# Window attention's order, and random features with 32-column stationary tiles, in an eight-stage hybrid network

## The reference, cut to what matters

```python
q = l2norm(q) * qs; k = l2norm(k) * ksc
q, k = rotary_xpos(q, k)
sim = einsum('bhwid,bhwjd->bhwij', bq * 8.0, bk)   # own window of 64 and the one before
mask = (i < j) | (i > j + WINDOW) | (j == -1)
out = einsum('bhwij,bhwjd->bhwid', softmax(where(mask, -max, sim)), bv)
x = x + out @ wo
```

```python
logits = einsum('bhld,hdf->bhlf', k, W0) - 0.5 * sum(k * k, -1)
alpha = softmax(logits over all l and f of a head)
N = einsum('bhlf,bhld->bhfd', alpha, v); D = sum(alpha, l)
phi = softmax(einsum('bhld,hdf->bhlf', q, W0), -1)
out = einsum('bhlf,bhfd->bhld', phi, N) / (einsum('bhlf,bhf->bhl', phi, D) + 1e-6)
```

## Time and profile before

| | |
|---|---|
| median of 3 runs | 6596.02 us (6581.57 to 6598.25) |
| profiled execution | 6608.01 us, its span 6606.2 us |
| busy PE, DVE, ACT, POOL | 5725.1, 3415.3, 3359.1, 2531.4 us |
| mean granted TensorE clock | 0.935 of 2.4 GHz |

### The profile page before, as it was taken

One profiled execution on the slowest core, in us unless ns is written; L12 is line 12 of the kernel. 1 busy time (PEld: TensorE's weight loads), 2 busy tenths in 40 slices (PEclk: granted clock), 3 DMA queues, 4 the chain that ended last, 5 costly groups with the idle time before them and its releaser, 6 DMA issues. The chain is left out here.

```text
span 6606.2 us, 126709 instructions
## 1 busy us (share of the span) xinstructions
PE 5725.1 (87%) x46071; PEld 3420.8 (52%) x46071; DVE 3415.3 (52%) x4087; ACT 3359.1 (51%) x5004; POOL 2531.4 (38%) x1721
## 2 busy tenths in 40 slices
PE   6876888888878988988998988998898998998998
PEld 2432555555535544553444554553446775676776
DVE  4557999999835544553435544554542112543112
ACT  4545888888834543544444443554343334332433
POOL 1223999999905524550215533551220000000000
PEclk8997999999989998999998999999998999888999
DMA  0002111111011101110001111110000000000000
GB/s 39 1 0 77 31 32 31 31 30 32 28 42 39 38 19 33 38 32 0 1 2 39 38 26 26 38 38 26 1 0 6 0 0 0 0 0 0 0 0 13
DMA packets 119695, 137.07 MB, mean 21 GB/s; under 512 B 31713, under 2 KB 85089, under 8 KB 118241
## 3 DMA queue, kind: packets, MB, share of 16 engines
q1 hardware_dynamic: 119520, 134.75, 7.3%
HBM read 46.55 MB, written 12.58 MB: 9 GB/s over the span
## 5 line engine op out<-in xcount | busy, mean ns | idle before, releaser
L2333 POOL TENSOR_TENSOR arena<-arena,wbig 128x1024 f32<-128x1024 f32 x512 | 1191.5, 2466 | 109.2 <-DMA wbig<-scratch_b 103.6
L2320 DVE TENSOR_TENSOR_SCAN arena<-banks,arena 128x1024 f32<-128x1024 f32 x512 | 1140.6, 2278 | 67.5 <-ACT banks L2264 49.2
L1510 POOL TENSOR_TENSOR arena<-arena 128x512 f32<-128x512 f32 x256 | 382.9, 1496 | 701.3 <-DMA arena<-arena 701.3
L768 POOL TENSOR_TENSOR X<-X,Z 128x1536 f32<-128x1536 f32 x2 | 9.5, 4760 | 1660.4 <-ACTq L761 1660.4
L601 DVE TENSOR_REDUCE arena<-banks 128x4 f32<-128x1024 f32 (+1 forms) x384 | 401.8, 1046 | 433.5 <-PE banks L435 305.3
L989 ACT ACTIVATE arena<-banks,wbig 128x512 f32<-128x512 f32 x512 | 351.6, 687 | 531.8 <-PE banks L946 522.9
L1021 DVE SCALAR_TENSOR_TENSOR arena<-banks,arena 128x128 f32<-128x128 f32 x512 | 144.1, 344 | 839.1 <-PE banks L930 839.1
L2264 ACT ACTIVATE banks<-banks 128x1020 f32<-128x1020 f32 x512 | 518.2, 1012 | 107.5 <-PE banks L2185 99.8
L2269 ACT COPY arena<-banks 128x1024 f32<-128x1024 f32 x512 | 520.8, 1017 | 51.1 <-POOL arena L2333 29.6
L547 ACT ACTIVATE Y<-banks 128x2048 f32<-128x2048 f32 x192 | 305.9, 1593 | 408.9 <-PE banks L471 311.5
L930 PEld LDWEIGHTS banks<-wbig,arena 128*128 128x128 f32 x4096 | 475.0, 192 | 53.6 <-issue 53.6
(11 more groups left out here) (297 smaller groups left out, 10848.1 us busy)
## 6 DMA issues: line engine op xcount, KB each, us to landing
arena<-arena SPq DMA_DIRECT2D x1024, 64.0 KB, 2.0
wbig<-scratch_d SPq DMA_DIRECT2D x512, 16.0 KB, 1.7
wbig<-scratch_b SPq DMA_DIRECT2D x64, 128.0 KB, 2.2
wbig<-scratch_c SPq DMA_DIRECT2D x64, 128.0 KB, 2.1
arena<-Z SPq DMA_DIRECT2D x64, 128.0 KB, 2.1
wbig<-in_l_ffn SPq DMA_DIRECT2D x1, 4185.0 KB, 12.9
X<-in_x SPq DMA_DIRECT2D x2, 2048.0 KB, 14.6
wbig<-in_l_ffn SPq DMA_DIRECT2D x1, 3879.5 KB, 11.8
```

Source lines behind the costliest of these rows:

```text
L1510: pool.tensor_tensor(half[g], half[g], sin_w, ALU.mult).then_inc(pool_f.sem, 1)
L2320: dve.tensor_tensor_scan(own, line(decay_bank[n % 2]), own, 0.0, ALU.mult, ALU.add)\
L2333: pool.tensor_tensor(four(h[par][:, m * 1024:m * 1024 + 1024]), four(us[n % 2]), Bs[par].unsqueeze(1).to_broadcast([128, 4, SEQ]), ALU.mult)\
```

## The change

In window attention, on PE `values_in(b+1)` is now issued at the end of the trip before, ahead of `turn(b+1, 0)`, and `maxima(b+1, 0)` after `values(b, 2)` and no longer before it. On DVE `reduce(b, 2)` goes ahead of `cosine(b+1, 0)` and `cosine(b+1, 1)`. ACT, POOL and SP keep their orders.

```diff
                 scores(b, par, 0)
-                values_in(b, par)
                 maxima(b, 1)
...
                 scores(b, par, 3)
                 if more:
                     spread_norms(b + 1, 1)
-                    maxima(b + 1, 0)
                 values(b, par, 2)
                 if more:
+                    maxima(b + 1, 0)
+                    values_in(b + 1, 1 - par)
                     turn(b + 1, 0)
...
             maxima(0, 0)
+            values_in(0, 0)
             turn(0, 0)
...
                     copy_raw(b + 1, 3)
+                reduce(b, 2)
+                if more:
                     cosine(b + 1, 0)
                     cosine(b + 1, 1)
-                reduce(b, 2)
-                if more:
                     clip(b + 1)
```

```diff
                 for c in range(2):
-                    to = bank[1][:, c * 128:(c + 1) * 128]
-                    pe.matmul(to, zt[:, c * 128:(c + 1) * 128], w["wv"], start=True, stop=False)
-                    last = pe.matmul(to, k.c["ones"][0:1, :], w["bv"][0:1, :], start=False, stop=True)
+                    last = pe.matmul(vbank[:, c * 128:(c + 1) * 128], zt[:, c * 128:(c + 1) * 128], w["wv"],
+                                     start=True, stop=True)
...
                 turn_features(1)
+                pe.wait_ge(dve_s.sem, dve_s.before(i, "ctx"))
...
+                pe.wait_ge(act_s.sem, act_s.at(i, "t0"))
+                feature_logits(kf, 0)
+                pe.wait_ge(act_s.sem, act_s.before(i, "ek1"))
+                for half in range(2):
+                    for c in range(2):
+                        for g in range(4):
+                            p = 4 * half + g
+                            last = pe.matmul(ntbank[rows(g), half * 128:(half + 1) * 128], v[:, c, p, :],
+                                             ak[c][:, p * 128:(p + 1) * 128], start=(c == 0), stop=(c == 1),
+                                             skip_group_check=True)
+                last.then_inc(pe_s.sem, 1)
+                pe.wait_ge(act_s.sem, act_s.at(i, "t1"))
+                feature_logits(kf, 1)
+                pe.wait_ge(act_s.sem, act_s.at(i, "ntc"))
+                for half in range(2):
+                    last = pe.transpose(bank[6][:, SEQ + half * 128:SEQ + (half + 1) * 128],
+                                        nts[:, half * 128:(half + 1) * 128], k.c["ident"])
...
-                pe.wait_ge(dve_s.sem, dve_s.at(i, "eps"))
+                pe.wait_ge(act_s.sem, act_s.at(i, "s1"))
+                pe.wait_ge(dve_s.sem, dve_s.at(i, "s2"))
+                for to, weight in ((obank, num_w), (dbank, den_w)):
+                    for b in range(2):
+                        for a in range(4):
+                            last = pe.matmul(to[rows(a), :], weight[:, a, b, :], pT[:, :, 2 * a + b, :],
+                                             start=(weight is num_w and b == 0), stop=True, skip_group_check=True)
+                last.then_inc(pe_s.sem, 1)
                 for c in range(2):
-                    for p in range(8):
-                        last = pe.matmul(obank[:, c, 2 * p:2 * p + 2, :].rearrange("p h d -> p (h d)"),
-                                         pT[c][:, p * 128:(p + 1) * 128], nn[:, p, :], start=True, stop=True)
...
                     pe.wait_ge(dve_s.sem, dve_s.at(i, f"sk{c}"))
                     feature_logits(qf, c)
...
+                act.wait_ge(pe_s.sem, pe_s.at(i, "nt"))
+                act.wait_ge(pe_s.sem, pe_s.before(i, "n"))
+                act.copy(nts, ntbank).then_inc(act_s.sem, 1)
                 act.wait_ge(pe_s.sem, pe_s.at(i, "n"))
+                act.wait_ge(dve_s.sem, dve_s.at(i, "sums"))
+                for h in range(2):
+                    half, cols = slice(64 * h, 64 * h + 64), slice(8 * h, 8 * h + 8)
+                    for b in range(2):
+                        last = act.copy(num_w[half, :, b, 16 * b + 8 * h:16 * b + 8 * h + 8], nbank[half, :, b, cols])
+                last.then_inc(act_s.sem, 1)
+                key_features(i, 0)
+                act.wait_ge(pe_s.sem, pe_s.at(i, "o"))
+                act.wait_ge(dve_s.sem, dve_s.before(i, "ctx"))
+                act.activation(recip, dbank, ACT.Ln).then_inc(act_s.sem, 1)
+                act.wait_ge(act_s.sem, act_s.at(i, "ln"))
+                act.activation(recip, recip, ACT.Exp, scale=-1.0).then_inc(act_s.sem, 1)
+                key_features(i, 1)
...
+                largest_key(i, 0)
+                dve.wait_ge(pe_s.sem, pe_s.at(i, "v"))
+                dve.wait_ge(pe_s.sem, pe_s.at(i, "nt"))
+                dve.tensor_tensor(v[:, :, :, 0:16], vbank.rearrange("p (c a d) -> p c a d", c=2, a=8),
+                                  bv.rearrange("p (a d) -> p a d", a=8).unsqueeze(1).to_broadcast([128, 2, 8, 16]),
+                                  ALU.add).then_inc(dve_s.sem, 1)
+                largest_key(i, 1)
...
+                dve.wait_ge(dve_s.sem, dve_s.at(i, "eps"))
+                dve.wait_ge(pe_s.sem, pe_s.before(i, "o"))
+                by_pair = sums.rearrange("p (a b h) -> p a b h", a=4, b=2)
+                for b in range(2):
+                    last = dve.tensor_copy(den_w[:, :, b, 16 * b:16 * b + 16].rearrange("p a (h d) -> p a h d", h=2),
+                                           by_pair[:, :, b, :].unsqueeze(3).to_broadcast([128, 4, 2, 8]))
+                last.then_inc(dve_s.sem, 1)
...
                 shift_queries(i, 0)
...
+                dve.wait_ge(act_s.sem, act_s.at(i, "rec"))
+                dve.tensor_tensor(out[:, tok(i, SEQ)], obank, recip, ALU.mult).then_inc(dve_s.sem, 1)
                 shift_queries(i, 1)
```

More of the change, by code:

```diff
@@ L1633, in random_feature_stage @@
     trips = BATCH + 1
[L1635 to L1639, removed]
+    pe_s = Steps(k, "products", ["q", "k", "t0", "v", "t1", "h2", "lk0", "nt", "lk1", "n", "mt", "z", "mb", "o", "lq0",
+                                 "lq1"], trips)
+    act_s = Steps(k, "lookups", ["eq0", "copy", "q", "k", "k2", "eq1", "t0", "t1", "ntc", "s1", "ek0", "ln", "rec",
+                                 "ek1"], trips)
+    dve_s = Steps(k, "vectors", ["h2", "mk0", "v", "mk1", "mks", "mk", "sums", "m1", "diag", "eps", "s2", "m", "sk0",
+                                 "sk1", "mq0", "sq0", "ctx", "mq1", "sq1"], trips)
     k.arena.reset()
     take = k.arena.take
-    zt, qf, kf, k2 = take(SEQ), take(SEQ), take(SEQ), take(SEQ)
-    v = take(2 * HEADS * VCOLS).rearrange("p (c h d) -> p c h d", c=2, h=HEADS)
+    zt, qf, kf, k2, nts, recip = (take(SEQ) for _ in range(6))
+    v = take(2 * 8 * 32).rearrange("p (c a d) -> p c a d", c=2, a=8)
+    bv = take(128)
     ak = [take(wide) for _ in range(2)]
     pq = [take(wide) for _ in range(2)]
-    pT = [take(wide) for _ in range(2)]
+    pT = take(2 * wide).rearrange("p (c a t) -> p c a t", c=2, a=8)
+    num_w, den_w = (take(8 * 32).rearrange("p (a b d) -> p a b d", a=4, b=2) for _ in range(2))
     mk = take(2 * HEADS).rearrange("p (c h) -> p c h", c=2)
@@ L1650, in random_feature_stage @@
     m = take(2 * HEADS).rearrange("p (c h) -> p c h", c=2)
[L1651 to L1654, removed]
+    mkb, m1, diag, sums = take(HEADS), take(1), take(HEADS), take(HEADS)
     bank = [k.psum[:, n, :] for n in range(8)]
[L1656 to L1660, removed]
+    vbank, zbank = bank[1][:, 0:SEQ], bank[1][:, SEQ:SEQ + HEADS]
+    ntbank = bank[6][:, 0:SEQ]
+    nbank = bank[6][:, SEQ:2 * SEQ].rearrange("p (a b d) -> p a b d", a=4, b=2)
+    hbank = bank[7][:, 0:32].rearrange("p (c h) -> p c h", c=2)
+    obank, dbank = bank[7][:, 0:SEQ], bank[7][:, SEQ:2 * SEQ]
+    own = w["own_head"].rearrange("p (h d) -> p h d", h=2)[:, :, HEAD_DIM]
     def logits(c):
@@ L1672, in spread, with rows, _ @@
         return ap.unsqueeze(2).to_broadcast([128, HEADS, FEATURES])
-    fills = [(v.rearrange("p c h d -> p (c h d)"), 1.0)] + [(buf, 1.0) for buf in ak + pq]
-    filled = Count(k, "filled", len(fills))
+    def rows(g):
+        return slice(32 * g, 32 * g + 32)
+    fills = [(v[:, :, :, 0:16], 0.0), (v[:, :, :, 16:18], 1.0), (v[:, :, :, 18:32], 0.0), (num_w, 0.0), (den_w, 0.0)]
+    fills += [(buf, 1.0) for buf in ak + pq]
+    filled = Count(k, "filled", len(fills) + 1)
+    biased = Count(k, "bias_spread", 1)
     with nc.Block() as block:
+        @block.tensor
+        def _(pe):
+            pe.matmul(vbank[:, 0:128], k.c["ones"][0:1, :], w["bv"][0:1, :], start=True, stop=True)\
+                .then_inc(biased.sem, 1)
         @block.vector
@@ L1680, in _ @@
                 dve.memset(buf, value).then_inc(filled.sem, 1)
-            dve.wait_ge(filled.sem, filled.at(len(fills)))
+            dve.wait_ge(biased.sem, biased.at(1))
+            dve.tensor_copy(bv, vbank[:, 0:128]).then_inc(filled.sem, 1)
+            dve.wait_ge(filled.sem, filled.at(len(fills) + 1))
     with nc.Block() as block:
@@ L1732, in _ @@
                 pe.transpose(bank[0][0:HEADS, 0:128], mkb, k.c["ident"]).then_inc(pe_s.sem, 1)
```

(21 more changed lines are left out.)

10 lines of the change are left out of this document (removed).

## The result

The changed kernel takes 6409.1 us, median of 4 runs (6401.3 to 6412.5), against 6597.1, the median of now 4 runs of the kernel before: ratio 0.9719 (0.9705 to 0.9734), 188 us less. The forecast was 110 less, and its range ended at 6430. The profiled execution's span is 6410.7 us.

A forecast was written before the change was run, and what follows sets the result against it. The prediction took TensorE's queue, in program order, to bound the kernel almost everywhere. Window attention 74 us less, random features 37 less and new fills 1 more made 110 off the 6596 median: 6486 us, range 6430 to 6555.

The forecast's parts named there:

- P: Window attention, PE: the start of the next batch's projection, from which the prediction counts times within a trip of 26.73 us.
- the clock: Random features: TensorE at half clock for 3.4 to 7 us a trip, about 2.2 us of it on the chain.
- that term's bound: Window attention: with every PE gap gone, a trip of 24.5 us, 132 us less over the four stages.
- The cycle of the window trip: Pool's chain to maxima(b+1, 0), 19.03 us, then PE's 7.70 to the next projection; forecast 25.5 us a trip, 74 less.
- the 1.23 us gap: Window attention: PE's wait ahead of turn(b, 2) for DVE's row maxima; slack, closing it alone would lengthen the 0.59 gap.
- The cosine's cover: Window attention: cosine 0, issued later under Pool's sin0, ends as before; otherwise add0 comes 0.88 us later, rival's chance 0.2.
- the chain: Random features: the serial steps of one trip across PE, DVE and ACT, 19.8 us; 22.0 with half clock, 37 us less.
- the 32-column blocks: Random features, PE: 32 passes of 128 columns in 1.08 us and 32 of 256 columns in 1.7 us.
- the sum that left out the drain: Random features: four tiling-mode changes a trip counted as free; at 0.2 us lost for each, 14 us smaller sum.
- Cosine 0 still near 1.8 us: Window attention, DVE: a sign of the forecast, cosine 0 keeping its duration, with add0 at 7.6 us after the projection's start.
- the terms of PE's work in random features: Random features: old numerators, bias pairs and transposes replaced by 32-column-tile passes and two transposes; some 5.5 us less a trip.
- 7.70 - 1.24: Window attention, PE: time from maxima(b+1, 0) to the next projection, less values(b, 2), which moves ahead of it.

The follow-up runs named there:

- e3: Changed kernel with PE's window order put back to that of the kernel before, leaving DVE's reduce(b, 2) move and the new random-feature stage: 6626.0 us.
- e2: Kernel before the change with only the random-feature part of the change, window stages as before: 6534.7 us, ratio 0.9902.
- e4: Changed kernel with DVE's reduce(b, 2) put back behind the two cosines, PE's moves kept: window trip 25.64 us, a window stage 431.3 us.
- e5: Changed kernel with the bf16 cast low0 made by DVE right behind qk1, no longer by Pool: 6371.4 us, ratio 0.9662.
- e7: Changed kernel with maxima(b+1, 0) put back ahead of values(b, 2), the other moves kept: 6569.2 us.
- e9: The changed kernel run again without any edit: 6413.1 us, ratio 0.9723.
- e6: Changed kernel with three superfluous products on PE ahead of the wait for the key maximum in random features: 6396.4 us, ratio 0.9705.
- e8: Changed kernel with values_in(b) put back behind scores(b, 0), the other moves kept: 6546.0 us.

## Why the prediction was too small

The direction and the mechanism held. The gain was 188 us and not 110, below the range's end at 6430, because four terms were too small, all on the same side: the window stages gave 107 us for 74 (the stretch from maxima 0 to P 25, the edges 7), the random-feature stage 59 for 37 (the clock), and stages without an edit, which the sum left out, some 22 for 0. The range had no case in which the window trip gains more than 1.23 us, though the prediction worked out 132 us as that term's bound.

**Right.** The cycle of the window trip: P to maxima(b+1, 0) was 19.03 us and still is, add0 stayed at P + 7.6, and the 1.23 us gap was slack, which e3 shows. The cosine's cover held. The random trip at full clock is 19.6 us where the chain gave 19.8, with the copies for den_w at 0.3, not 0.2; the 32-column blocks took 1.08 and 1.93 us against 1.08 and 1.7. The change of tiling mode left no gap in the matmul records: the blocks follow their neighbours within 0.1 us, so the sum that left out the drain of the Trainium skill (TensorEngine Tiling (Array Packing), Key Properties), tried there with 14 us, was nearer.

Two readings were wrong without touching the sum. "Cosine 0 still near 1.8 us" contradicts the reasoning above it: issued 0.8 us later and ending where it did, it takes 1.02. And the terms of PE's work in random features give 8.0 - 3.2 = 4.8 us less a trip, not 5.5.

**Wrong, the stretch from maxima 0 to P.** The term "7.70 - 1.24" should have been 6.46 and measured 2289.50 - 2283.46 = 6.04: 0.42 us a trip, 25 us in 60 trips. Between turn(b+1, 0) and the products that need ACT's shift there are 1.03 us now and were 1.37. PE and ACT, before and then after:

```profile
2340.26 0.38 ACT L1356 ACTIVATE arena<-banks 128x256 f32<-128x256 f32 x1 [2.89 <-PE banks L1244]
...
2340.99 0.46 ACT L1363 ACTIVATE arena<-banks,cst 128x256 bf16<-128x256 f32 x1
2341.51 0.31 PE L1224 MATMUL banks<-arena,cstb 64*128 64x192 bf16 x4 [0.15 <-ACT arena L1363]
```

```profile
2286.21 0.47 ACT L1364 ACTIVATE arena<-banks,cst 128x256 bf16<-128x256 f32 x1 [2.52 <-PE banks L1209]
2286.74 0.31 PE L1224 MATMUL banks<-arena,cstb 64*128 64x192 bf16 x4
```

In the kernel before, ACT was in the reciprocal of pair 2, released by values(b, 2) just ahead of the turn, and began the shift 0.85 us behind it; now it begins 0.50 us behind. That values(b, 2), right ahead of the turn, also sat in ACT's way I had not counted. The stretch is 1.37 us in e2 too, and 1.03 in e4, e5 and e7; in e7 values(b, 2) is again behind maxima 0, but values_in lies between it and the turn. So this is 0.34 of the 0.42 us. The rest is small steps between neighbours on PE (maxima 0 and values_in 0.08 and 0.10 shorter, one later step 0.09 longer), which I leave open.

**Wrong, the edges.** 60 trips of 1.67 us are 100 of the 107 us (101, added up in the traces). I had given what a stage has outside its 15 trips from one projection to the next nothing; it gave 1.6 to 1.8 us a stage.

**Wrong, the clock in random features.** I put 2.2 us of half clock on each trip. It falls in about two of three trips (11 of 16 here, 10 of 16 in e9) and costs mostly 1.3 to 1.7 us there: 20.5 to 20.7, not 22.0. That is 22 us of the miss; e6 shows the mechanism and its size. The mean clock of the stage is 0.94, not 0.8 to 0.9, which is 2.3 to 2.7 us at half clock a trip, not 3.4 to 7.

**Outside the sum.** Some 22 to 29 us came from stages without an edit. The prediction put them at nothing without a reason. Over the profiles, the start took 1951 to 1964 us and the first expert stage 1100 to 1115, with no edit that orders them; the changed kernel's two profiles differ by 5.5 us in the start alone. What follows the random features took 607.8 us in both profiles with the old random-feature stage, and 595 to 602 in eleven of twelve with the new one (610.5 in e5), so some 10 us may belong to that stage. The medians say that part of the gain is steady: 188, against 166 in the touched stages. Where the clock falls in those stages may depend on when they begin; no run here settles it.

## What to carry to other kernels

Write a trip as a cycle, with the engine, the DMA and the wait that each stretch belongs to: a gap on the busiest engine is worth its length only if the cycle goes through it, and moves around one cycle must be judged together. Two short waits of TensorE with some 9 us of work between them cost nothing here, where one of about the same total, or two with 0.7 us between them, brought its clock down for microseconds; so before closing a gap ask where the slack will gather. Where an idle stretch ahead of heavy products can't be removed, harmless products in it can pay.

## What the runs showed of the hardware

With a wait of 1.9 us in each trip, TensorE fell from 2.4 to 1.2 GHz in most trips (54 of 60 in e3, 44 of 60 in e7), with 25.6 of 28 us busy; waits of 1.23, 0.59 and 0.28 us in one trip didn't bring it down, and 0.67 and 0.98 us with 0.7 us of work between did in many trips (38 of 60 in e8, mean clock 0.94). The Trainium skill (SBUF — State Buffer, Who interferes with whom) has an exclusive lock between DVE and Pool; the runs agree: a cosine of 0.68 us alone takes up to 1.81 behind a Pool op and ends 0.55 us behind it whether issued 1.26 or 0.47 us ahead of that op's end, and Pool's 1.27 us become 1.52 to 1.79 where they meet a cosine.
